# Two orders swapped in a normalise-and-feed-forward stream: centring before the mean on TensorE, squaring before the logarithm on ScalarE

## The chip, the cores and the metric

The kernel runs on one core of one Trainium2 chip. The metric is the time of one execution on the device, in microseconds. Five engines matter: TensorE (PE, matmuls into PSUM), VectorE (DVE), ScalarE (ACT), GpSimd (POOL) and SyncE (SP, which only starts transfers here). Each works off its own instructions in order, and they meet through semaphores.

## The reference, cut to what matters

The input is `x`, 16 images of 48 channels and 64 x 64 pixels, f32. There are two layers, each with a convolution-like mixer and a feed-forward part on the tokens (pixels):

```
x = x + L0_conv(ln_c(x))          # one of 4 experts: depthwise 3x3, gelu, 1x1
t = t + L0_ffn(ln_t(t))           # 48 -> 192 -> 48, relu, values rounded to an 8-bit and a 16-bit float
x = x + L1_conv(ln_c(x))          # cosine transform, layer norm, a state-space scan on four quarters, transform back
t = t + L1_ffn(ln_t(t))
```

Both `ln_c` and `ln_t` normalise each pixel over its 48 channels: `(v - mean(v)) / sqrt(var(v) + eps)`. The feed-forward part of either layer, and the norm in front of the first layer's mixer, are what the change is in.

## The kernel before

Two images of 48 channels make a pair on 96 partitions, so there are eight pairs (`PAIRS`), each 96 x 4096. A hardware loop runs over seven of them (`pair(p, False)`), and the last stands behind it (`pair(7, True)`). In a pair the second layer's mixer is computed (turning, cosine transform, scan, transform back), with the expert convolution of the next pair woven into the scan. After it comes a **stream**, the piece that the change touches.

A stream works through chunks of 512 pixels (`CH`), eight to an image pair. In a pair of the loop it has 24 of them: eight of the second layer's feed-forward (`ffn1`, source `x`), eight of the next pair's first feed-forward (`ffn0`, source `col`), and eight of the norm of the pair after that (`norm`, source `xin`). The stream of the last pair has eight (`ffn1`). In front of the loop there is one of eight (`norm`) and one of 16 (`ffn0`, `norm`). So 200 chunks are normalised in all.

Each chunk goes through these steps; the numbers are lines of the profile:

- TensorE multiplies it by `centre` (identity less the mean over channels), L547, into PSUM bank 0 or 1 (`LN_DEPTH` = 2 banks): the centred values.
- ScalarE squares them, L880, into `sq`.
- TensorE multiplies `sq` by `average`, L540, into PSUM bank 2 or 3: the variance.
- ScalarE takes the logarithm, L869, and `exp(-0.5 * .)` of it, L874: the inverse root.
- VectorE multiplies the centred values by it: L1191 in a feed-forward chunk (into `xq8`, 8 bits), L1199 in a norm chunk, there with a sum over the chunk, L1202. This counts up `normed`.
- In a feed-forward chunk TensorE applies the first layer, L559, three matmuls into banks 4 to 6. ScalarE copies them out, L887. VectorE adds the bias and clips, L1212 and L1214, and rounds to 8 bits, L1231. TensorE applies the second layer, L570, bank 7. VectorE copies it out, L1183, and adds its bias, L1222. GpSimd adds the residual, L1403.
- In the last iterations of a stream with `ffn0`, blocks of the new `x` are centred and turned: L523 on TensorE (eight matmul records a block), L856 and L857 on ScalarE.

The order is written out by hand. Each engine has its own function `stream`, a loop over `t` in which step k of the chain is done for chunk `t - k`, so that several chunks are under way. VectorE's iteration is L1183 of t-4, L1191 or L1199 of t-1, L1212 and L1214 of t-2, L1222 of t-4, L1231 of t-2. Waits are written as `wait_ge(semaphore, count)`, with `n = n0 + t` counting chunks over the whole kernel. The wait of the centring on `normed` guards its PSUM bank:

```
pe.wait_ge(normed, n - LN_DEPTH + 1)
```

For chunk t it asks that chunk t-2 has been multiplied. `settled` is a no-operation behind a group of waits.

Of the kernel before, what the change touches and what calls it, by code (L numbers as in the profile page):

```python
# [18 lines left out]
ACT = mybir.ActivationFunctionType  # L19
# [3 lines left out]
R = 2 * C  # L23
PX = H * W
PAIRS = B // 2
CH = 512
NCH = PX // CH
# [38 lines left out]
LN_DEPTH = 2  # L66
# [6 lines left out]
def program(nc, a):  # L73
# [3 lines left out]
    def sb(name, shape, dt=F32):  # L77
        return ctx.enter_context(nc.sbuf_tensor(name, shape, dt))

    def sem(name):  # L80
        return ctx.enter_context(nc.semaphore(name))

    with ctx:

        ident = sb("ident", [128, 128])
        centre = sb("centre", [R, R])
# [51 lines left out]
        def cut(rows, n, dt=F32, at=None):  # L138

            if at is None:  # L140
                at = top[0]
                top[0] += n
            v = arena[0:rows, at:at + n]
            return v if dt == F32 else v.bitcast(dt)
# [5 lines left out]
        sq = cut(R, LN_DEPTH * CH).rearrange("p (b n) -> p b n", b=LN_DEPTH)  # L150
# [50 lines left out]
        ps = ctx.enter_context(nc.psum_tensor("ps", [128, 8, 512], F32))  # L201
# [23 lines left out]
        centred = sem("centred")  # L225
        squared = sem("squared")
        averaged = sem("averaged")
        logged = sem("logged")
        rstd_ready = sem("rstd_ready")
        normed = sem("normed")  # L230
# [114 lines left out]
        def turned_in(parts, t):  # L345

            n = t - len(parts) + 6
            return n if "ffn0" in parts and 0 <= n < NG else None

        def is_ffn(parts, t):  # L350
            return 0 <= t < len(parts) and parts[t] != "norm"
# [30 lines left out]
        def settled(eng):  # L382


            eng.nop(nofuse=True)
# [111 lines left out]
        def _(pe):  # L497
# [7 lines left out]
            def turn_in(P, n):  # L505

                c = IN_ORDER[n]
                if n == 0:
                    pe.wait_ge(hf_ready, P * 2 * NCH + NCH)
                if n == 3:  # L510
                    pe.wait_ge(yf_ready, P * 2 * NCH + NCH)
                if n >= 4:
                    pe.wait_ge(pix_act, P * ACT_PAIR + act_before(T_IN) + n - 3)
                    settled(pe)
                    pe.wait_ge(ln_act, P * LN_ACT + A_SQUARE + n - 4)
                    settled(pe)
                if n == 4:
                    pe.wait_ge(centre_ready, P + 1)
                    settled(pe)
                pe.wait_ge(ffn_done, P * 2 * NCH + c + 1)  # L520
                for g in range(GB):
                    px = (c * GB + g) * 128
                    mm = pe.matmul(ps[:, 4 + n % 4, g * R:(g + 1) * R], x[:, px:px + 128], centre[:],  # L523
                                   start=True, stop=True)
                mm.then_inc(pix_ps, 1)
                if n == 1:

                    pe.wait_ge(ln_act, P * LN_ACT + A_SQUARE)
                    pe.matmul(centre_ps, sel_centre[:], pix[:, GRP // 2, :], start=True,
                              stop=True).then_inc(cen_ps, 1)  # L530

            def stream(n0, f0, parts, ready, src, P):

                for t in range(len(parts) + 3):
                    if 0 <= t - 1 < len(parts):
                        j, n = (t - 1) % NCH, n0 + t - 1
                        pe.wait_ge(squared, n + 1)
                        if not (parts[0] == "norm" and t - 1 < LN_DEPTH):
                            pe.wait_ge(logged, n - LN_DEPTH + 1)
                        pe.matmul(ps[0:R, LN_DEPTH + j % LN_DEPTH, :], average[:], sq[:, j % LN_DEPTH, :],  # L540
                                  start=True, stop=True).then_inc(averaged, 1)
                    if t < len(parts):
                        j, n = t % NCH, n0 + t
                        ready(t)
                        if not (parts[0] == "norm" and t < LN_DEPTH):
                            pe.wait_ge(normed, n - LN_DEPTH + 1)
                        pe.matmul(ps[0:R, j % LN_DEPTH, :], centre[:], src[parts[t]][:, j * CH:(j + 1) * CH],  # L547
                                  start=True, stop=True).then_inc(centred, 1)
                    if is_ffn(parts, t - 2):
                        j = t - 2  # L550
                        layer = int(parts[j] == "ffn1")
                        pe.wait_ge(normed, n0 + j + 1)
                        if j == 0:
                            ready(NCH - 1)
                        if j > 0:
                            pe.wait_ge(hf_ready, f0 + j)
                        settled(pe)
                        for b in range(3):
                            mm = pe.matmul(ps[:, 4 + b, :], w1[:, layer, b, :], xq8[:, j % 2, :],  # L559
                                           start=True, stop=True)  # L560
                        mm.then_inc(fc1_ready, 1)
                    if is_ffn(parts, t - 3):
                        j = t - 3
                        layer = int(parts[j] == "ffn1")
                        pe.wait_ge(h8_ready, f0 + j + 1)
                        if j > 0:
                            pe.wait_ge(yf_ready, f0 + j)
                        settled(pe)
                        for b in range(3):
                            mm = pe.matmul(ps[0:R, 7, :], w2[:, layer, b, :],  # L570
                                           h8[:, j % 2, b * CH:(b + 1) * CH],
                                           start=(b == 0), stop=(b == 2))
                        mm.then_inc(fc2_ready, 1)
                    if turned_in(parts, t) is not None:
                        turn_in(P, turned_in(parts, t))
# [30 lines left out]

            pe.wait_ge(x_in, 16)
            stream(0, 0, ("norm",) * NCH, lambda t: None, {"norm": xin}, None)
            router(1)
            pe.wait_ge(expert_ready, 1)  # L610
            for t in range(NCH + 1):
                if t < NCH:
                    if t >= 4:
                        pe.wait_ge(gelu_ready, t - 3)
                    for k in range(TAPS):
                        mm = pe.matmul(ps[0:R, t % 4, :], diag[:, k, :],
                                       taps_of(padded[:, t * ROWS:t * ROWS + ROWS + 2, :], k),
                                       start=(k == 0), stop=(k == TAPS - 1))
                    mm.then_inc(taps_ps, 1)
                if t >= 1:  # L620
                    j = t - 1
                    pe.wait_ge(gelu_ready, j + 1)
                    if j >= 4:
                        pe.wait_ge(pwb_ready, j - 3)
                    pe.matmul(ps[0:R, 4 + j % 4, :], pw_gated[:], gel0[:, j % 2, :],
                              start=True, stop=True).then_inc(pw_ps, 1)
# [216 lines left out]
        def _(act):  # L843
# [15 lines left out]
            def stream(n0, f0, parts, P):  # L859

                for t in range(len(parts) + 2):
                    if 0 <= t - 1 < len(parts):
                        k, n = (t - 1) % LN_DEPTH, n0 + t - 1
                        e = int(parts[t - 1] != "norm")
                        old = not (parts[0] == "norm" and t - 1 < LN_DEPTH)
                        act.wait_ge(averaged, n + 1)
                        if old:
                            act.wait_ge(rstd_ready, n - LN_DEPTH + 1)
                        act.activation(lnv[:, k, :], ps[0:R, LN_DEPTH + k, :], ACT.Ln,  # L869
                                       bias=eps[0:R, e:e + 1]).then_inc(logged, 1)  # L870
                        act.wait_ge(logged, n + 1)
                        if old:
                            act.wait_ge(normed, n - LN_DEPTH + 1)
                        act.activation(rstd[:, k, :], lnv[:, k, :], ACT.Exp, scale=-0.5).then_inc(rstd_ready, 1)  # L874
                    if t < len(parts):
                        k, n = t % LN_DEPTH, n0 + t
                        act.wait_ge(centred, n + 1)
                        if not (parts[0] == "norm" and t < LN_DEPTH):
                            act.wait_ge(averaged, n - LN_DEPTH + 1)
                        act.activation(sq[:, k, :], ps[0:R, k, :], ACT.Square).then_inc(squared, 1)  # L880
                    if is_ffn(parts, t - 2):

                        j = t - 2
                        act.wait_ge(fc1_ready, f0 + j + 1)
                        if j >= 2:
                            act.wait_ge(hr_ready, 2 * (f0 + j - 1))
                        act.activation(hf[:, j % 2, :], ps[:, 4:7, :].rearrange("p b n -> p (b n)"),  # L887
                                       ACT.Copy).then_inc(hf_ready, 1)
                    if turned_in(parts, t) is not None:
                        turn_in(P, turned_in(parts, t))  # L890
# [25 lines left out]
            for t in range(NCH + 1):  # L916
# [6 lines left out]
                if t >= 1:  # L923
                    j = t - 1
# [683 lines left out]
```

## Time and profile before

| | |
|---|---|
| three runs, median (lowest to highest) | 4641.31 us (4617.7 to 4661.02) |
| profiled execution | 4614.75 us, of which the span from first to last instruction is 4612.9 |
| busy: TensorE, VectorE, ScalarE, GpSimd | 87%, 77%, 64%, 54% of the span |
| mean granted TensorE clock | 0.922 of full speed |
| chunks in all streams | 200 (8, 16, seven times 24, 8) |

"Busy" is time in which an instruction of the engine was running. A start in the timeline is the moment at which its waits are over. An f32 matmul of 512 columns shows as two records, so 200 means are 400 records of L540.

### The profile page before, as it was taken

To read this page: it belongs to the slowest core of one execution; us is meant where nothing else is said; L and a number is where in the kernel's file an instruction comes from. 1 tells how busy PE (TensorE), PEld (TensorE's weight loads), DVE (VectorE), ACT (ScalarE), POOL (GpSimd) and SP (SyncE) were. 2 spreads that over 40 slices of the span, in tenths; PEclk is the share of its full clock that TensorE was granted. 3 is DMA by queue.
4 is the path that set the end of the run, shared out by engine and by line. 5 is a ranking of instruction groups with operands and counts; after the bars stand their busy time and mean duration, and the time that the engine had idled before them with its cause. 6 is when DMAs were issued, how large, how long until landed. Compare 5 with 4: busy or idle time off the path is not lost.

```text
span 4612.9 us, 49417 instructions
## 1 busy us (share of the span) xinstructions
PE 4009.5 (87%) x14248; PEld 1461.2 (32%) x14248; DVE 3563.9 (77%) x3093; ACT 2959.8 (64%) x3572; POOL 2483.7 (54%) x1148
## 2 busy tenths in 40 slices
PE   6779986899869998699986999779997799868997
PEld 2322233322332223322243222432233222332223
DVE  1469967699668996599965998659977699667996
ACT  2567756677566766577665675667757677565664
POOL 0237742577416873177731777227752477425774
PEclk9889998899989999799997999979999899987888
DMA  1147741577316763277623775347751577406661
GB/s 41 42 115 185 175 118 43 150 175 185 92 45 173 179 169 76 64 184 173 159 69 83 177 179 133 83 101 174 184 134 44 125 187 173 112 15 148 160 158 51
DMA packets 166836, 580.22 MB, mean 126 GB/s; under 512 B 22460, under 2 KB 23208, under 8 KB 162952
## 3 DMA queue, kind: packets, MB, share of 16 engines
q1 hardware_dynamic: 152168, 538.66, 47.6%
q10 hardware_dynamic: 14336, 37.76, 2.8%
q8 instruction: 132, 2.16, 0.2%
q14 instruction: 200, 1.64, 0.1%
HBM read 467.12 MB, written 71.48 MB: 117 GB/s over the span
## 4 chain that ended last, share of the span: by engine, by line
PE 56%; DVE 18%; issue 14%; ACT 8%; DMA 2%; POOL 1%; DVEq 0%; SPq 0%; ACTq 0%; POOLq 0%
PE ps L725 12%; PE ps L744 7%; PE ps L790 6%; DVE ps L1357 6%; PE ps L679 5%; DVE arena L1362 5%; PE ps L597 3%; PE ps L540 3%; PE ps L753 2%; PE ps L736 2%; PE ps L703 2%; PE ps L711 2%; ACT arena L887 2%; PE ps L695 2%; PE ps L687 2%
## 5 line engine op out<-in xcount | busy, mean ns | idle before, releaser
L1449 POOL TENSOR_TENSOR arena<-arena 128x1024 f32<-128x1024 f32 x768 | 1855.7, 2422 | 745.4 <-DVE arena L1362 744.8
L1362 DVE TENSOR_TENSOR_SCAN arena<-arena,ps 128x1024 f32<-128x1024 f32 x768 | 1756.1, 2287 | 98.4 <-ACT arena L1050 3.4
L1050 ACT ACTIVATE arena<-arena,a_all 128x1024 f32<-128x1024 f32 x768 | 873.0, 1141 | 340.7 <-DVE arena L1362 246.9
L1357 DVE TENSOR_TENSOR ps<-ps,arena 128x1024 f32<-128x1024 f32 x768 | 930.3, 1211 | 147.1 <-PE ps L727 146.2
L725 PE MATMUL ps<-arena,spread 32*128 32x512 f32 x1536 | 897.4, 672 | 96.7 <-DVE arena L1362 71.8
L727 PE MATMUL ps<-arena,spread 32*128 32x512 f32 x1536 | 883.6, 673 | 0.0
L744 PE MATMUL ps<-arena,gather 128*32 128x512 f32 x3072 | 536.4, 647 | 3.3 <-POOL arena L1449 2.3
L790 PE MATMUL ps<-x 96*96 96x512 f32 x1008 | 498.5, 612 | 0.0
L725 PEld LDWEIGHTS ps<-arena,spread 32*128 32x128 f32 x1536 | 233.0, 190 | 727.7 <-issue 420.2
L679 PE MATMUL ps<-arena,w_in 96*96 96x512 f32 x512 | 289.7, 718 | 37.0 <-DMA arena<-xq 37.0
L1403 POOL TENSOR_TENSOR x<-x,arena 96x512 f32<-96x512 f32 x64 | 113.9, 1780 | 369.1 <-DVE arena L1222 369.1
L1015 ACT ACTIVATE arena<-ps 128x512 f32<-128x512 f32 x128 | 76.4, 597 | 311.7 <-PE ps L711 311.7
L790 PEld LDWEIGHTS ps<-x 96*96 96x96 f32 x1008 | 143.1, 162 | 331.5 <-issue 331.5
L540 PE MATMUL ps<-arena,average 96*96 96x512 f32 x400 | 218.9, 629 | 30.8 <-ACT arena L880 30.8
L845 ACT ACT_TABLE_LOAD x178 | 228.4, 1283 | 23.9 <-DMA wo<-in_wo 20.7
L1439 POOL TENSOR_TENSOR arena<-arena 96x1024 f32<-96x1024 f32 x64 | 150.8, 2357 | 164.3 <-DVE arena L1347 164.3
L744 PEld LDWEIGHTS ps<-arena,gather 128*32 128x32 f32 x3072 | 107.8, 115 | 395.1 <-issue 312.7
L727 PEld LDWEIGHTS ps<-arena,spread 32*128 32x128 f32 x1536 | 227.7, 190 | 0.0
L1347 DVE TENSOR_TENSOR arena<-arena 96x1024 f32<-96x1024 f32 x64 | 76.8, 1199 | 186.4 <-ACT arena L1036 186.4
L869 ACT ACTIVATE arena<-ps,eps 96x512 f32<-96x512 f32 x200 | 136.4, 682 | 125.2 <-PE ps L540 125.2
L1429 POOL MEMSET arena<- 96x6 f32 x8 | 0.8, 103 | 400.5 <-ACT xq L966 400.5
L1191 DVE TENSOR_TENSOR arena<-ps,arena 96x512 fp8e5<-96x512 f32 x128 | 86.9, 679 | 128.6 <-ACT arena L874 128.3
(160 smaller groups left out, 5758.2 us busy)
## 6 DMA issues: line engine op xcount, KB each, us to landing
arena<-dl SPq DMA_DIRECT2D x768, 512.0 KB, 5.3
dl<-arena ACTq DMA_DIRECT2D x64, 384.0 KB, 5.1
x<-pn SPq DMA_DIRECT2D x56, 247.5 KB, 5.0
arena<-in_x SPq DMA_DIRECT2D x9, 1536.0 KB, 14.7
arena<-xq SPq DMA_DIRECT2D x64, 192.0 KB, 6.1
arena<-arena ACTq DMA_DIRECT2D x64, 192.0 KB, 4.7
out<-x SPq DMA_DIRECT2D x64, 192.0 KB, 2.1
arena<-xq SPq DMA_DIRECT2D x64, 191.8 KB, 5.4
```

The costliest lines, as they stand in the source:

```text
L540: pe.matmul(ps[0:R, LN_DEPTH + j % LN_DEPTH, :], average[:], sq[:, j % LN_DEPTH, :], start=True, stop=True).then_inc(averaged, 1)
L679: mm = pe.matmul(ps[0:DI, 6 + c, :], w_in[:, q, j, :], xs[:, i, c * 512 + 2 * j:c * 512 + 2 * j + 512], start=(j == 0), stop=(j == 1))
L725: pe.matmul(ps[:, bank, :], spread[rows[0], r, :], u[rows[0], i, 0:512], start=True, stop=True)
L727: pe.matmul(ps[:, bank + 1, :], spread[rows[1], r, :], u_low[rows[1], i, :], start=True, stop=True).then_inc(ubc_ready, 1)
L744: mm = pe.matmul(ps[b * BLK:(b + 1) * BLK, c, :], gather[:, r, :], hs[:, (r * TRIO + b) % HSS, c * 512:(c + 1) * 512], start=False, stop=( ...
L790: mm = pe.matmul(ps[0:R, 7, :], diag[:, k, :], taps_of(win[:, v % 2], k), start=(k == 0), stop=(k == TAPS - 1), skip_group_check=True)
L845: exp_table = lambda: act.preload_act_table_set("natural_log_exp_and_others")
L1050: act.activation(da[:, m % DAS, :], dbc[:, m % DBC, :], ACT.Exp, scale=a_all[:, v // 2, m:m + 1]).then_inc(da_ready, 1)
L1357: dve.tensor_tensor(driven, driven, bmat[:, v % 2, :], ALU.mult).then_inc(bu_ready, 1)
L1362: dve.tensor_tensor_scan(hs[:, m % HSS, :], da[:, m % DAS, :], driven, 0.0, ALU.mult, ALU.add).then_inc(h_ready, 1)
L1439: pool.tensor_tensor(u[:, i, :], delta, xi[:, i, :], ALU.mult).then_inc(u_ready, 1)
L1449: pool.tensor_tensor(product, product, cmat[:, v % 2, :], ALU.mult).then_inc(pr_ready, 1)
```

## The change

On TensorE the centring of chunk t, with its waits, is put in front of the mean of chunk t-1. On ScalarE the square of chunk t, with its waits, is put in front of the logarithm and root of chunk t-1. VectorE, GpSimd and SyncE are left as they are, and so are all the waits themselves.

```
@@ tensor: stream
                 for t in range(len(parts) + 3):
+                    if t < len(parts):
+                        j, n = t % NCH, n0 + t
+                        ready(t)
+                        if not (parts[0] == "norm" and t < LN_DEPTH):
+                            pe.wait_ge(normed, n - LN_DEPTH + 1)
+                        pe.matmul(ps[0:R, j % LN_DEPTH, :], centre[:], src[parts[t]][:, j * CH:(j + 1) * CH],
+                                  start=True, stop=True).then_inc(centred, 1)
                     if 0 <= t - 1 < len(parts):
                         j, n = (t - 1) % NCH, n0 + t - 1
                         pe.wait_ge(squared, n + 1)
...
                         pe.matmul(ps[0:R, LN_DEPTH + j % LN_DEPTH, :], average[:], sq[:, j % LN_DEPTH, :],
                                   start=True, stop=True).then_inc(averaged, 1)
-                    if t < len(parts):
...
-                        pe.matmul(ps[0:R, j % LN_DEPTH, :], centre[:], src[parts[t]][:, j * CH:(j + 1) * CH],
-                                  start=True, stop=True).then_inc(centred, 1)
@@ scalar: stream
                 for t in range(len(parts) + 2):
+                    if t < len(parts):
+                        k, n = t % LN_DEPTH, n0 + t
+                        act.wait_ge(centred, n + 1)
+                        if not (parts[0] == "norm" and t < LN_DEPTH):
+                            act.wait_ge(averaged, n - LN_DEPTH + 1)
+                        act.activation(sq[:, k, :], ps[0:R, k, :], ACT.Square).then_inc(squared, 1)
                     if 0 <= t - 1 < len(parts):
...
                         act.activation(rstd[:, k, :], lnv[:, k, :], ACT.Exp, scale=-0.5).then_inc(rstd_ready, 1)
-                    if t < len(parts):
-                        k, n = t % LN_DEPTH, n0 + t
...
-                        act.activation(sq[:, k, :], ps[0:R, k, :], ACT.Square).then_inc(squared, 1)
```

## Rows read from the trace of the kernel before

**Rows 1.** The page's part 4, chain that ended last: shares of the span by engine.

```profile
PE 56%; DVE 18%; issue 14%; ACT 8%; DMA 2%; POOL 1%; DVEq 0%; SPq 0%; ACTq 0%; POOLq 0%
```

**Rows 2.** Busy time by engine around one stream; PEclk is the granted clock.

```profile
670.00:787.00 117.00, 87.04 (x359) 45.24 (x357) 85.44 (x163) 78.32 (x117) 31.45 (x20) 0.93 0.20 57
```

**Rows 3.** Timeline, feed-forward part: start, us, engine, line; idle before it and releaser.

```profile
701.36 0.68 ACT L869 ACTIVATE arena<-ps,eps 96x512 f32<-96x512 f32 x1 [0.73 <-PE ps L540]
...
702.46 0.68 DVE L1183 CAST arena<-ps 96x512 f16<-96x512 f32 x1
...
703.24 0.82 PE L570 MATMUL ps<-arena,w 128*96 128x512 fp8e5 x3 [0.41 <-DVE arena L1183]
703.89 0.59 PE L540 MATMUL ps<-arena,average 96*96 96x512 f32 x1
...
704.75 1.02 PE L547 MATMUL ps<-col,centre 96*96 96x512 f32 x2
...
704.96 0.68 ACT L869 ACTIVATE arena<-ps,eps 96x512 f32<-96x512 f32 x1 [0.44 <-PE ps L540]
...
705.67 0.63 ACT L874 ACTIVATE arena<-arena 96x512 f32<-96x512 f32 x1
706.21 0.57 ACT L880 ACTIVATE arena<-ps 96x512 f32<-96x512 f32 x1
...
706.68 1.44 ACT L887 ACTIVATE arena<-ps 128x1536 f16<-128x1536 f32 x1
...
708.15 0.48 DVE L1212 TENSOR_SCALAR arena<-arena,b 128x1024 f16<-128x1024 f16 x1 [0.53 <-ACT arena L887]
...
709.95 0.68 DVE L1183 CAST arena<-ps 96x512 f16<-96x512 f32 x1
```

**Rows 4.** Timeline, the start of the same stream, its first chunk.

```profile
675.35 1.10 PE L540 MATMUL ps<-arena,average 96*96 96x512 f32 x2 [0.76 <-ACT arena L880]
...
676.29 1.02 PE L547 MATMUL ps<-x,centre 96*96 96x512 f32 x2
...
676.49 0.68 ACT L869 ACTIVATE arena<-ps,eps 96x512 f32<-96x512 f32 x1 [1.19 <-PE ps L540]
677.21 0.63 ACT L874 ACTIVATE arena<-arena 96x512 f32<-96x512 f32 x1
...
677.94 0.69 DVE L1191 TENSOR_TENSOR arena<-ps,arena 96x512 fp8e5<-96x512 f32 x1 [3.48 <-ACT arena L874]
```

**Rows 5.** Timeline, norm part of the same stream, its last two chunks.

```profile
755.43 0.68 ACT L869 ACTIVATE arena<-ps,eps 96x512 f32<-96x512 f32 x1 [0.42 <-PE ps L540]
...
756.15 0.63 ACT L874 ACTIVATE arena<-arena 96x512 f32<-96x512 f32 x1
...
756.81 0.69 DVE L1199 TENSOR_TENSOR arena<-ps,arena 96x512 f32<-96x512 f32 x1 [1.61 <-ACT arena L874]
...
758.45 0.68 ACT L869 ACTIVATE arena<-ps,eps 96x512 f32<-96x512 f32 x1 [0.42 <-PE ps L540]
```

**Rows 6.** Timeline behind that stream: a matmul that waits for VectorE.

```profile
769.27 0.27 DVE L1240 TENSOR_SCALAR pool_lhs<-pool_mask,pooled 96x96 f32<-96x96 f32 x1
...
769.59 0.48 PE L580 MATMUL ps<-router_w,pool_lhs 96*96 96x4 f32 x2 [9.43 <-DVE pool_lhs L1240]
```

**Rows 7.** Timeline of the first stream of all (norm chunks only).

```profile
32.19 0.68 ACT L869 ACTIVATE arena<-ps,eps 96x512 f32<-96x512 f32 x1 [2.11 <-PE ps L540]
...
34.54 2.02 PE L540 MATMUL ps<-arena,average 96*96 96x512 f32 x2 [0.68 <-ACT arena L880]
...
36.36 1.91 PE L547 MATMUL ps<-arena,centre 96*96 96x512 f32 x2
...
36.60 0.68 ACT L869 ACTIVATE arena<-ps,eps 96x512 f32<-96x512 f32 x1 [2.11 <-PE ps L540]
```

**Rows 8.** Timeline of TensorE in the scan of the last pair.

```profile
4358.18 0.81 PE L725 MATMUL ps<-arena,spread 32*128 32x512 f32 x1 [1.41 <-DVE arena L1362]
...
4358.78 1.06 PE L725 MATMUL ps<-arena,spread 32*128 32x512 f32 x1
```

More of the change, by code:

```diff
@@ L541, in stream @@
                                   start=True, stop=True).then_inc(averaged, 1)
-                    if t < len(parts):
[L543 to L546, printed above, removed]
-                        pe.matmul(ps[0:R, j % LN_DEPTH, :], centre[:], src[parts[t]][:, j * CH:(j + 1) * CH],
-                                  start=True, stop=True).then_inc(centred, 1)
                     if is_ffn(parts, t - 2):
@@ L874, in stream @@
                         act.activation(rstd[:, k, :], lnv[:, k, :], ACT.Exp, scale=-0.5).then_inc(rstd_ready, 1)
-                    if t < len(parts):
-                        k, n = t % LN_DEPTH, n0 + t
-                        act.wait_ge(centred, n + 1)
-                        if not (parts[0] == "norm" and t < LN_DEPTH):
-                            act.wait_ge(averaged, n - LN_DEPTH + 1)
-                        act.activation(sq[:, k, :], ps[0:R, k, :], ACT.Square).then_inc(squared, 1)
                     if is_ffn(parts, t - 2):
```

## The prediction

> **What bounds the kernel now.** I read the page's chain of waits first [rows 1]: it runs through TensorE for 56% of the span, through VectorE for 18% and through ScalarE for 8%, so it changes engine all the time and the bound differs by stage. The diff touches `stream` alone, so I went on to the busy times around one stream and saw 87 of 117 us on TensorE, 85 on VectorE and 78 on ScalarE, at a granted clock of 0.93 [rows 2]. Nobody is full there, so a ring of waits sets the pace, and the timeline has to be walked.
>
> In the feed-forward part [rows 3] I start at a VectorE copy of the second layer's output (L1183, at 702.46) and follow what waits for what. The second layer's matmuls start 0.78 later (703.24). Behind them in TensorE's order stands the mean (L540, 703.89: 0.65). Its logarithm starts at 704.96 (1.07), the root at 705.67 (0.71), the square of the next chunk at 706.21 (0.54), the copy of the first layer's output (L887) 0.47 after that, the VectorE steps on that copy at 708.15 (1.47), and the next but one L1183 at 709.95 (1.80). One turn takes 709.95 - 702.46 = 7.49 us and covers two chunks: 3.745 us a chunk. In the norm part a shorter ring binds, that of mean, logarithm, root, square and mean: logarithm to logarithm is 758.45 - 755.43 = 3.02 us [rows 5].
>
> The square does stand in both rings, and its centred input is there before ScalarE comes to it. That is what the change addresses.
>
> **What it changes.** No instruction is added or removed: there are 200 centring matmuls, 200 means, 200 squares, logarithms and roots before and after. The orders change. ScalarE now does square(t), logarithm(t-1), root(t-1). TensorE now does centre(t), mean(t-1). No DMA moves, and the queues of SyncE and GpSimd stay as they are. The wait that matters moves with the matmul: centre(t) waits for normed(t-2), since the centred values lie in two PSUM banks. Before, mean(t-1) stood ahead of that wait. Now it stands behind it, and so do the first layer of chunk t-2 and the second layer of chunk t-3.
>
> That closes a new ring with a period of one chunk: centre(t), mean(t-1), logarithm(t-1), root(t-1), the VectorE multiply of chunk t-1, centre(t+1). Its links come from the rows:
> - centre to mean: 0.94, the distance of two such matmuls of which the first found TensorE idle (675.35 to 676.29) [rows 4]. Both are 512 columns of f32 on 96 rows. With TensorE busy it would be 0.86 (703.89 to 704.75) [rows 3], but the centring always waits here.
> - mean to logarithm: 1.07, the mean coming right behind other matmuls [rows 3].
> - logarithm to root: 0.71 [rows 3]. Root to multiply: 0.73 in the feed-forward part (677.21 to 677.94) [rows 4], 0.66 in the norm part (756.15 to 756.81) [rows 5].
> - multiply to centring: 0.74. The multiply takes 0.69. The handover from VectorE to TensorE is not shown for this pair, so I take the nearest row, 0.05 (769.27 + 0.27 to 769.59) [rows 6]. The 0.78 of L1183 to L570 [rows 3] has a settling nop in it and is the upper end.
>
> The sum is 4.19 us a chunk in the feed-forward part and 4.12 in the norm part. Bounds: 4.11 with 0.86 for the first link, 4.23 with 0.78 for the last.
>
> Does something else end later? I lay one turn out from centre(t) = 0. Mean 0.94; the square is ready to run at 1.14 (the delay behind a lone matmul, 675.35 to 676.49) [rows 4] and frees ScalarE at 1.61; logarithm 2.01; root 2.72; multiply 3.45; L887 at 2.72 + 0.54 = 3.26; the steps on it at 4.73; L1183 at 6.53. It leads to the next multiply 0.60 later, at 7.13, against the 7.64 that the ring asks for. The second layer starts at 6.53 - 4.19 + 0.78 = 3.12 and is over at 3.77, before 4.19. Everything fits with some 0.4 us to spare, so the new ring is the bound. The old ring does not shrink either: its square (0.54) leaves and a centring (0.86) enters, because the second layer is now followed by centre and only then by mean. That gives 7.49 - 0.54 + 0.86 = 7.81, or 3.9 a chunk, above 3.745 as well.
>
> Now the sum, logarithm to logarithm:
> - A full stream (24 chunks, seven of them) takes 758.45 - 676.49 = 81.96 us now. The first logarithm stays where it is. After it come 16 turns of 4.19 (67.04) and 6 of 4.12 (24.72). The last chunk has no centring ahead of its mean. Its logarithm follows when TensorE has turned one more block and ScalarE has done its root and the two copies of that block, about 2.0. Together 93.8, so +11.8 each, **+82.7** in all.
> - The stream in front of the loop (16 chunks) has eight feed-forward turns fewer: 11.8 - 8 x (4.19 - 3.745) = **+8.2**, an estimate that leaves out a short slow stretch at its start.
> - The last stream (8 chunks, feed-forward only) takes 701.36 - 676.49 = 24.87 for its seven distances [rows 3, 4]. Six turns of 4.19, then 2.83 (the last mean waits for the second layer, 3.77 - 0.94) make 27.97: **+3.1**.
> - The first stream of all (8 norm chunks) runs on slow matmuls, 1.82 apart, with 2.06 from mean to logarithm and 4.41 a chunk [rows 7]. Its new ring is 1.82 + 1.99 + 0.71 + 0.66 + 0.74 = 5.92, where 1.99 is 2.06 less the 0.07 by which 1.07 is under 1.14. That is six times +1.51; about 0.9 at the start, since the first mean now follows two centrings (3.64) and not one and its square (2.06 and some 0.6); and 1.8 in place of 4.41 for the last: **+7.3**.
>
> This is +101 us. What could hide it? The streams stand between stages that all wait for their last chunk: VectorE goes on with its large sums as soon as the last chunk is normed. The spill of `x` and the store of the normed image are issued from the stream's own events and have the following stage to land. I count no cover.
>
> **The clock.** The matmuls of the stream take 0.59 us (or 1.02 for two) [rows 3, 4], the upper of the two levels (2.4 GHz); those of rows 7 take 1.91 for two, the lower (1.2 GHz). In the last scan a matmul pair that came after an idle time of 1.41 us took 0.81 us, and the one behind it 1.06 [rows 8]: the clock had fallen to the lower level. In a new stream TensorE idles 0.7 and 0.4 in each turn of the feed-forward part, and some 1.5 us a turn in the norm part (centre, mean and eight turning matmuls fill 2.6 of 4.12). At the start, before any first layer, the second mean waits about 2.4 us. So I expect the clock to fall at the start of about half of the streams, one turn each at the lower level, and dense matmuls to bring it back: 4 x 1.8 = +7. The bounds of this term are 0 and the second rival below. The Trainium skill (TensorE: Matmul & The Clock Gate, Why this matters for your kernels) warns only of idle gaps longer than any of these; by its rule the term is nothing and the sum ends at +101. The fall behind a 1.41 us gap speaks against relying on it.
>
> **Forecast.** 101 + 7 = 108 us. The profiled execution took 4614.75, of which the span is 4612.9, and would become 4723. The median of the three runs is 27 above that, at 4641, so the forecast is 4749, slower by 2.3%.
>
> **Rivals.**
> 1. *The ring with the square is cut and nothing takes its place* (faster). The feed-forward ring would lose 0.54: 6.95 / 2 = 3.48 a chunk, 0.27 less on some 120 turns, -32. The norm part would go from 3.02 to TensorE's own 2.65 (two times 0.86 and a block of turning matmuls, 0.9) on some 50 turns, -18. Time 4591. Against it is the wait on `normed` ahead of centre(t), and the sum of its ring. It decides if that ring is shorter than 3.745, and no link has 0.45 us to give. 4%.
> 2. *The clock falls in the norm part and stays.* Then a norm turn costs 5.92 and not 4.12: 1.8 x 6 in eight streams is +86, time 4835. For it: idle gaps of 1.5 us each turn, just the size of that in rows 8, and the first stream of all, which never left slow matmuls while turning at 4.41 [rows 7]. Against it: the norm part holds the full clock now, and eight turning matmuls fill every turn. A partial form of it, two or three turns in some streams, gives 4780. 20% together.
> 3. *The delay is taken up outside the streams or the change does not act* (within 1%, at most 4687). A wait on a transfer or a branch at the end of the stream would have to hide 60 of 101 us. All eight stages behind a stream begin with work on its last chunk. 6%.
> 4. *The handovers are quicker than my rows* and the old ring of 3.9 binds: 0.28 less on 120 feed-forward turns, -34, time 4715. It lies inside the forecast's range.
>
> **Chances.** Forecast with rival 4 70%, rival 2 20%, rival 3 6%, rival 1 4%. The range goes from 4700 (rival 4 and some of the 43 us over which the runs before spread) to 4820, which takes in half of rival 2. A measurement of this kernel tells about 1% from no change. Faster by over 1%: 0.04. Within 1%: 0.06. Slower by over 1%: 0.90.
>
> **What would show it.** Right: logarithms 4.1 to 4.2 us apart in both parts of a stream, a full stream of about 94 us, the centring matmul with an idle time before it that ends with the multiply (L1191 or L1199), and the mean 0.94 behind it. Wrong: a distance of 3.5 (rival 1) or 3.9 (rival 4); matmul durations of 1.0 to 1.1 us in the norm part (rival 2); a span that grows by much less than the streams do (rival 3). What would spoil the forecast is a clock that behaves otherwise at gaps of 1.5 to 2.4 us, or a shift of the scans by some us that changes their own clock.

## The result, and the profile after

The changed kernel takes 4789.92 us in the median of four runs (4780.93 to 4801.09), the kernel before 4630.19 in its four (4617.7 to 4661.02). The ratio is 1.0336, 95% interval 1.0275 to 1.0397: slower by 3.4%, or 160 us. The forecast was 4749 us, with a range of 4700 to 4820. The profiled execution took 4793.87 us with a span of 4792.1, against 4614.75 and 4612.9 before: 179 us more. Its mean granted clock is 0.899, against 0.922.

Three parts of the page answer to [rows 1]: the busy times, the chain of waits by engine, and two of the costliest groups with the idle time ahead of them.

```profile
PE 4118.4 (86%) x14248; PEld 1489.8 (31%) x14248; DVE 3570.8 (75%) x3093; ACT 2983.2 (62%) x3572; POOL 2487.4 (52%) x1148
...
PE 59%; DVE 17%; issue 12%; ACT 8%; DMA 2%; POOL 1%; DVEq 0%; SPq 0%; POOLq 0%; ACTq 0%
...
L867 ACT ACTIVATE arena<-ps 96x512 f32<-96x512 f32 x200 | 118.4, 592 | 244.9 <-PE ps L540 244.9
L1191 DVE TENSOR_TENSOR arena<-ps,arena 96x512 fp8e5<-96x512 f32 x128 | 87.9, 686 | 232.9 <-ACT arena L880 232.9
```

The counts are those of before, so no work was added. The multiply L1191 now waits 232.9 us for the root (L880), where it waited 128.3 before, and the square L867 waits 244.9 us for the centring (L540), where it waited 68.3. The groups of centring matmuls by source and shape say what those wait for:

```profile
L540 PE MATMUL ps<-x,centre 96*96 96x512 f32 x128 | 74.4, 676 | 44.5 <-DVE arena L1191 44.5
L540 PE MATMUL ps<-col,centre 96*96 96x512 f32 x128 | 73.8, 662 | 31.6 <-DVE arena L1191 29.3 <-POOL col L1410 2.3
L540 PE MATMUL ps<-arena,centre 96*96 96x512 f32 x144 | 90.8, 718 | 61.3 <-DVE arena L1199 49.8 <-DVE arena L1191 6.5 <-DMA arena<-in_x 5.1
```

That is 137 us of idle TensorE, nearly all of it ended by the multiply (L1191 or L1199); before, the centring followed on 7 us in all, none of it ended by the multiply. The centring matmuls are also longer than at full clock: a record of one on `x` took 592 ns before and takes 676 now, a mean over two clock levels.

The timeline of the first full stream shows both effects. The five rows from 697.86 are its start, the seven from 735.44 the feed-forward part (beside [rows 3]), and the last five the norm part (beside [rows 5]).

```profile
697.86 0.68 ACT L875 ACTIVATE arena<-ps,eps 96x512 f32<-96x512 f32 x1 [0.33 <-PE ps L547]
...
699.31 0.69 DVE L1191 TENSOR_TENSOR arena<-ps,arena 96x512 fp8e5<-96x512 f32 x1 [3.48 <-ACT arena L880]
...
700.14 1.96 PE L540 MATMUL ps<-x,centre 96*96 96x512 f32 x2 [2.31 <-DVE arena L1191]
...
701.89 1.91 PE L547 MATMUL ps<-arena,average 96*96 96x512 f32 x2
...
703.84 0.68 ACT L875 ACTIVATE arena<-ps,eps 96x512 f32<-96x512 f32 x1 [1.11 <-PE ps L547]
...
735.44 0.68 ACT L875 ACTIVATE arena<-ps,eps 96x512 f32<-96x512 f32 x1 [0.27 <-PE ps L547]
...
736.16 0.63 ACT L880 ACTIVATE arena<-arena 96x512 f32<-96x512 f32 x1
...
736.52 0.82 PE L570 MATMUL ps<-arena,w 128*96 128x512 fp8e5 x3 [0.47 <-DVE arena L1183]
...
736.92 0.69 DVE L1191 TENSOR_TENSOR arena<-ps,arena 96x512 fp8e5<-96x512 f32 x1 [0.50 <-ACT arena L880]
...
737.66 1.10 PE L540 MATMUL ps<-col,centre 96*96 96x512 f32 x2 [0.32 <-DVE arena L1191]
...
738.60 1.02 PE L547 MATMUL ps<-arena,average 96*96 96x512 f32 x2
...
739.65 0.68 ACT L875 ACTIVATE arena<-ps,eps 96x512 f32<-96x512 f32 x1 [0.27 <-PE ps L547]
...
784.51 1.10 PE L540 MATMUL ps<-arena,centre 96*96 96x512 f32 x2 [1.29 <-DVE arena L1199]
...
785.45 1.84 PE L547 MATMUL ps<-arena,average 96*96 96x512 f32 x2
...
787.33 0.68 ACT L875 ACTIVATE arena<-ps,eps 96x512 f32<-96x512 f32 x1 [1.09 <-PE ps L547]
...
789.45 2.02 PE L540 MATMUL ps<-arena,centre 96*96 96x512 f32 x2 [0.50 <-DVE arena L1199]
...
793.21 0.68 ACT L875 ACTIVATE arena<-ps,eps 96x512 f32<-96x512 f32 x1 [1.12 <-PE ps L547]
```

Read one turn from 735.44 on. The root follows the logarithm by 0.72, the multiply the root by 0.76, the centring the multiply by 0.74, the mean the centring by 0.94, and the next logarithm the mean by 1.05. The sum is 4.21 us, where one chunk took 3.745 before. This is the ring that was forecast, link by link. The second layer (L570) starts inside it and ends none of its waits.

At the start of the stream the same ring runs on slow matmuls: centring and mean take 1.96 and 1.91 us (two records each), and the logarithms are 703.84 - 697.86 = 5.98 apart. In the norm part the clock falls during the mean at 785.45 (1.84), and the logarithms are 793.21 - 787.33 = 5.88 apart. The windows over these three stretches show the granted clock in the column behind POOL's:

```profile
696.00:710.00 14.00, 10.65 (x16) 2.89 (x15) 3.08 (x5) 6.52 (x10) 0.00 (x0) 0.65 0.19 46
713.00:775.00 62.00, 49.03 (x144) 16.44 (x143) 46.72 (x89) 47.23 (x59) 25.05 (x14) 1.00 0.09 26
785.00:803.00 18.00, 17.00 (x42) 9.61 (x41) 4.96 (x10) 8.87 (x16) 1.99 (x2) 0.51 0.16 54
```

A clock of 1.00 is the upper level (2.4 GHz), 0.51 the lower (1.2 GHz). TensorE seems full in the third window (17.00 of 18.00 us), yet only because each matmul lasts nearly twice as long.

From each stream's first logarithm to its last, all streams together took 683.6 us before and take 837.8 now: +154 of the +179. A full stream took 81.96. Two of the seven now take 96.8, the other five 99.3 to 104.6.

### The profile page after: what moved, and what is told of

Same layout as the page of the kernel before. It is cut to its first block, busy times and chain, and to the rows that moved or that the text cites. A ratio compares the mean times of both kernels' runs of the same rounds, so it can differ in the third digit from the quotient of the medians.

```text
span 4792.1 us, 49417 instructions
## 1 busy us (share of the span) xinstructions
PE 4118.4 (86%) x14248; PEld 1489.8 (31%) x14248; DVE 3570.8 (75%) x3093; ACT 2983.2 (62%) x3572; POOL 2487.4 (52%) x1148
## 4 chain that ended last, share of the span: by engine, by line
PE 59%; DVE 17%; issue 12%; ACT 8%; DMA 2%; POOL 1%; DVEq 0%; SPq 0%; POOLq 0%; ACTq 0%
PE ps L725 11%; PE ps L744 7%; PE ps L790 6%; DVE ps L1357 6%; PE ps L679 5%; PE ps L540 5%; DVE arena L1362 4%; PE ps L547 4%; PE ps L597 3%; ACT arena L875 3%; PE ps L753 2%; ACT arena L880 2%; PE ps L703 2%; PE ps L736 2%; PE ps L711 2%
## 5 line engine op out<-in xcount | busy, mean ns | idle before, releaser
L867 ACT ACTIVATE arena<-ps 96x512 f32<-96x512 f32 x200 | 118.4, 592 | 244.9 <-PE ps L540 244.9
L1191 DVE TENSOR_TENSOR arena<-ps,arena 96x512 fp8e5<-96x512 f32 x128 | 87.9, 686 | 232.9 <-ACT arena L880 232.9
L547 PE MATMUL ps<-arena,average 96*96 96x512 f32 x400 | 238.8, 683 | 0.0
```

## The experiments

Each kernel was timed against the kernel before on the same chip. "Streams" is the sum over all ten streams of the time from first to last logarithm, from the profiled execution. In the edits, `centre(t)` and the like stand for the statements of that step.

**TensorE's swap alone.** The kernel before with centre(t) ahead of mean(t-1) in TensorE's order; ScalarE as before.

```diff
 for t in range(len(parts) + 3):      # TensorE
+    centre(t)      # waits for normed(t-2)
     mean(t-1)
-    centre(t)
```

> Only TensorE's order is changed (centring of t ahead of the mean of t-1); ScalarE keeps logarithm, root, square. Theory: the new ring is centre(t), mean(t-1), logarithm, root, multiply, centre(t+1), and ScalarE's order is no part of it. So this edit alone gives nearly the whole loss: logarithms 4.2 us apart in the feed-forward part and 4.1 in the norm part, time 4740 to 4800, as the full change. Rival: the loss needs the square ahead of the logarithm (ScalarE waiting for the centring before it does the logarithm); then this kernel stays within 1% of the 4630 before, or in the middle at about 4700.

It took 4817.74 us, a ratio of 1.0419 (1.0375 to 1.0464), 18 us above the range that I expected. The feed-forward logarithms are 4.21 to 4.28 apart, as in the full change, so the moved wait alone makes the ring. The norm distances are 4.12 at full clock, but mostly 5.89 (here at the lower level):

```profile
786.48 0.68 ACT L869 ACTIVATE arena<-ps,eps 96x512 f32<-96x512 f32 x1 [2.40 <-PE ps L547]
...
788.60 2.02 PE L540 MATMUL ps<-arena,centre 96*96 96x512 f32 x2
...
790.41 1.91 PE L547 MATMUL ps<-arena,average 96*96 96x512 f32 x2
...
792.36 0.68 ACT L869 ACTIVATE arena<-ps,eps 96x512 f32<-96x512 f32 x1 [3.31 <-PE ps L547]
```

The streams sum to 877.6 us, more than in the full change (837.8), since the clock is low for more of the norm turns. Added to this, ScalarE's swap takes nothing from the ring. It shortens the last distance of a stream (1.99 against 3.01 at full clock).

**ScalarE's swap alone.** The kernel before with square(t) ahead of logarithm(t-1) and root(t-1) in ScalarE's order; TensorE as before.

```diff
 for t in range(len(parts) + 2):      # ScalarE
+    square(t)      # waits for centred(t)
     logarithm(t-1); root(t-1)
-    square(t)
```

> Only ScalarE's order is changed (square of t ahead of the logarithm of t-1); TensorE keeps mean, centre. Theory: the logarithm of t-1 now waits for the square of t and so for the centring of t, which TensorE does behind the mean. Norm part: ring centre, square, logarithm, root, multiply, centre = 1.07 + 0.47 + 0.71 + 0.66 + 0.74 = 3.65 us a chunk. Feed-forward part: the old ring with 0.86 + 1.07 + 0.47 in place of 1.07 from mean to logarithm, less the square, is about 8.35 for two chunks, 4.18 each. Over 120 and 48 chunks that is +52 and +30, time 4700 to 4740. Rival: squaring early only helps, since the centred input was waiting (the intent of the change); then 4630 or less.

It took 4784.45 us, a ratio of 1.034 (1.0302 to 1.0379), well above the 4700 to 4740 expected. The feed-forward part came as expected: the distances alternate between 4.38 and 3.97, a mean of 4.175. The norm part did not. In all seven full streams its last full turns are 5.07 apart, behind two of about 7.1 and 5.5. In the one below, the clock fell behind an idle time of 1.84 us in which TensorE waited for a VectorE copy (L1183), at the change from feed-forward to norm. The timeline of one such turn, and the windows ahead of it and over it:

```profile
773.55 0.67 ACT L875 ACTIVATE arena<-ps,eps 96x512 f32<-96x512 f32 x1
...
774.47 1.92 PE L540 MATMUL ps<-arena,average 96*96 96x512 f32 x2
...
776.17 1.91 PE L547 MATMUL ps<-arena,centre 96*96 96x512 f32 x2
777.88 1.86 PE L523 MATMUL ps<-centre,x 96*128 96x96 f32 x8
...
778.62 0.67 ACT L875 ACTIVATE arena<-ps,eps 96x512 f32<-96x512 f32 x1
```

```profile
715.00:760.00 45.00, 34.32 (x110) 13.23 (x107) 34.28 (x65) 34.26 (x44) 19.52 (x11) 1.00 0.09 27
765.00:790.00 25.00, 25.00 (x62) 14.24 (x62) 6.43 (x12) 11.91 (x25) 2.43 (x3) 0.50 0.20 65
```

Mean, centring and turning start 1.70, 1.71 and 1.65 apart and fill the turn: at the lower level TensorE itself is the bound. It is busy for 25.00 of 25.00 us and the clock does not come back. In the 16-chunk stream the clock stayed up, and there the distance was 3.74, close to the ring of 3.65 that I had worked out. So the ring was right and the clock was the miss, as in the prediction itself. This swap loses by another ring than the full change: the logarithm of t-1 waits behind the square of t, and so for a centring that TensorE does behind the mean.

**A third bank for the centred values.** The full change, but centred chunks rotate through three PSUM banks, and the fourth holds every mean. centre(t) now waits for normed(t-3), and mean(t-1) for the logarithm before it. The control is the kernel before with the same banks.

```diff
-pe.wait_ge(normed, n - LN_DEPTH + 1)     # centre(t)
-pe.matmul(ps[0:R, j % LN_DEPTH, :], ...)
+pe.wait_ge(normed, n - 3 + 1)
+pe.matmul(ps[0:R, t % 3, :], ...)
-pe.wait_ge(logged, n - LN_DEPTH + 1)     # mean(t-1)
-pe.matmul(ps[0:R, LN_DEPTH + j % LN_DEPTH, :], ...)
+pe.wait_ge(logged, n)
+pe.matmul(ps[0:R, 3, :], ...)
```

> The changed kernel with three PSUM banks for centred chunks (0 to 2) and one for the mean (3), so that the centring of t waits for the multiply of t-3 and not t-2. Theory: this cuts the new ring. The feed-forward part then runs at the old ring with a centring in place of the square, 3.9 us a chunk (+20 over the kernel before), the norm part at 2.7 (-15), and the long idle time of TensorE at the start of a stream is gone. Time 4620 to 4660. Rival: the loss comes from the means standing later in TensorE's order or from the clock by itself; then the third bank takes back less than half of the 160 us, time over 4710.

> Control: the kernel before with the same three banks for centred chunks and one for the mean. Theory: no ring that bounds it goes through a centred bank or a second mean bank, so nothing changes: logarithms 3.745 and 3.02 us apart, time 4615 to 4650. Rival: the bank layout is worth something by itself (then it is faster or slower by over 1%, and the kernel with the new orders and three banks has to be read against this one).

The changed orders with three banks took 4617.11 us, a ratio of 0.9978 (0.9955 to 1.0001). The control took 4633.03, 1.0008 (0.9989 to 1.0027), with the distances of before. The expected ranges were 4620 to 4660 and 4615 to 4650. One bank more gives the whole loss of the change back and gives nothing to the old order. It is the wait on `normed`, at a depth of two, that costs. In the timeline the centring comes well ahead of its use:

```profile
698.80 1.02 PE L541 MATMUL ps<-col,centre 96*96 96x512 f32 x2
699.66 1.02 PE L548 MATMUL ps<-arena,average 96*96 96x512 f32 x2
700.73 0.68 ACT L876 ACTIVATE arena<-ps,eps 96x512 f32<-96x512 f32 x1 [0.27 <-PE ps L548]
700.97 0.68 DVE L1184 CAST arena<-ps 96x512 f16<-96x512 f32 x1
701.75 0.82 PE L571 MATMUL ps<-arena,w 128*96 128x512 fp8e5 x3 [0.42 <-DVE arena L1184]
702.40 1.02 PE L541 MATMUL ps<-col,centre 96*96 96x512 f32 x2
...
704.33 0.68 ACT L876 ACTIVATE arena<-ps,eps 96x512 f32<-96x512 f32 x1 [0.27 <-PE ps L548]
...
708.59 0.68 ACT L876 ACTIVATE arena<-ps,eps 96x512 f32<-96x512 f32 x1 [0.27 <-PE ps L548]
```

TensorE now waits for L1184, the copy of the second layer's output. The distances alternate, 3.60 and 4.26: the old feed-forward ring with the square out and a centring in, at the 3.9 a chunk of the prediction's layout. The norm part goes down to 2.58 (a full stream also has one turn of 2.81 and one of 3.48), and the first stream takes 14.39 us in place of 30.87. The streams sum to 665.9 us, 18 less than before. But 16.5 of these 18 are the first stream, and mostly its clock: a mean took 1.02 to 1.17 us there, against 2.02 before [rows 7]. A full stream takes 82.4 us, no less than the 81.96 of before. In the profiled executions the time outside the streams is 18 us longer, so that nothing is left in the end.

**TensorE kept busy: four kernels against the clock.** To separate the clock from the ring I gave TensorE work that changes no result. In the first, the turning blocks 0 to 4 of a stream's norm part are done twice into the same place. In the second, two more centrings follow the first mean and one follows the second, into a bank that nobody reads before it is written again. The third has both.

```diff
-for g in range(GB):
+for g in tuple(range(GB)) * (2 if n <= 4 else 1):     # turning
 ...
     mean(t-1)
+    for _ in range(3 - t):     # t is 1 or 2; not in the stream of norm chunks alone
+        pe.matmul(ps[0:R, 7, :], centre[:], src[parts[0]][:, 0:CH], start=True, stop=True)
```

> The changed kernel, with the eight matmuls of each of the turning blocks 0 to 4 of a stream done twice into the same bank before they are reported (0.86 us more work in each of five norm turns; the result is the same). The ring of the norm part does not run through them and has 1.5 us of idle TensorE time a turn. Theory: it is this idle time that lets the clock fall near the end of five of the seven full streams; with 0.65 left the clock holds, all norm distances are 4.12 and not up to 5.9, and the last one is 1.99 in all streams. That takes 22 us off the profiled streams: time 4755 to 4775, faster than the changed kernel in spite of more work. Rival: the clock falls for another reason and the extra work only costs; then 4790 or more.

> The changed kernel, with two matmuls of 0.86 us into an unused bank behind the first mean of a stream with a feed-forward part, and one behind the second mean (nothing reads them). Theory: the idle time of 2.3 us between the first mean and the third centring makes the clock fall in all eight such streams; with it filled, the first two distances of a stream are 4.2 to 4.3 each and not 5.0 to 6.0. About 2.3 us a stream, 19 in all: time 4765 to 4780. Rival: the clock falls later, at the second or third turn, where some 1.7 us are still idle; then only the place of the slow turns moves and the time stays at 4790.

> The changed kernel with both fillers, at the start of each stream and in five norm turns. Theory: inside the streams the clock then stays at its upper level, a full stream takes about 96 us in all seven places, and what is left against the 82 us before is the ring alone. If only the streams count: 4735 to 4755. Rival: the time saved in a stream comes back in the stage behind it, whose own clock depends on when the stream ends, as the start filler alone has shown (16 us less in the streams of the profiled run, none in the time); then 4765 to 4785.

With turning doubled: 4773.19 us, 1.0306 (1.0273 to 1.0339). In the eight streams that have turning blocks every norm distance is 4.12 and every last one 1.99, for one turn of 5.5 instead of 4.6; the streams sum to 820.1. With the start filled: 4795.46, 1.0344 (1.031 to 1.0379). The first distances are 4.25 (4.18 in the 16-chunk stream) and the streams sum to 821.9, but the time did not follow, against what I expected (4765 to 4780): outside the streams the profiled execution is 16 us longer than the change (3970.7 against 3954.2). With both: 4748.85, 1.0249 (1.0216 to 1.0282), all seven full streams alike at 96.3 us, 801.0 in sum. The windows of the third kernel, the first two in the places of those after the change, the last over the end of the same stream:

```profile
696.00:710.00 14.00, 11.70 (x31) 3.94 (x31) 5.06 (x9) 9.31 (x13) 0.00 (x0) 1.00 0.14 34
713.00:775.00 62.00, 49.89 (x157) 18.16 (x156) 46.31 (x88) 45.51 (x58) 26.36 (x15) 1.00 0.09 27
775.00:793.00 18.00, 16.62 (x93) 11.50 (x92) 6.43 (x12) 12.38 (x23) 2.15 (x2) 1.00 0.28 90
```

The first window has a clock of 1.00 where the change had 0.65, the last 1.00 where the change had 0.51 at the end of its stream. The kernel with 187 more matmuls in it (374 records) is 41 us faster than the change, which is the clock's part that such fillers can take back, net of their own cost. What is left over the kernel before is 113 us.

The fourth kernel goes the other way: the mean stands behind the first layer, so that a feed-forward turn holds 0.65 us more for the same work.

```diff
     centre(t)
-    mean(t-1)
     first_layer(t-2)
+    mean(t-1)
     second_layer(t-3)
```

> The changed kernel with the mean of t-1 put one step later still on TensorE, behind the first layer of t-2 (0.64 us of matmuls at the full clock). Nothing else moves. Theory: the new ring takes in whatever TensorE does between centring and mean, so each feed-forward turn grows by 0.65, from 4.2 to 4.85, and the norm turns, which have no first layer, stay at 4.12. About 120 turns: +78 on the 4790 of the changed kernel, 4850 to 4880. Rival: the ring is not what sets the pace in the feed-forward part (a ring through the second layer or the output copies is); then the 0.65 is hidden in TensorE's idle time of 1.1 us a turn and the time stays at 4790.

It took 4940.03 us, 1.0645 (1.0592 to 1.0698).

```profile
746.49 1.10 PE L540 MATMUL ps<-col,centre 96*96 96x512 f32 x2 [1.03 <-DVE arena L1191]
...
748.08 1.02 PE L560 MATMUL ps<-arena,average 96*96 96x512 f32 x2
749.14 0.68 ACT L875 ACTIVATE arena<-ps,eps 96x512 f32<-96x512 f32 x1 [0.91 <-PE ps L560]
...
754.00 0.68 ACT L875 ACTIVATE arena<-ps,eps 96x512 f32<-96x512 f32 x1 [0.92 <-PE ps L560]
...
756.56 1.51 PE L540 MATMUL ps<-col,centre 96*96 96x512 f32 x2 [1.32 <-DVE arena L1191]
```

The distance at full clock is 4.86 = 4.21 + 0.65: whatever stands between centring and mean is paid in full, as it must be in a ring. The time came out above what I expected (4850 to 4880): the clock now falls in the feed-forward part too, where slow turns of 6.2 to 7.3 us stand among those of 4.9, behind idle times of about 1 us in each turn (1.03 ahead of the centring here, then 1.32 ahead of the first slow one). The streams sum to 970.9 us.

**The feed-forward ring of before, shortened.** Both kernels have two FFN steps moved: TensorE's second layer runs at t-4 instead of t-3, and VectorE multiplies chunk t-1 ahead of its copy of the second layer's output. The first keeps the orders and banks of before; the second has the changed orders and three banks.

```diff
-if is_ffn(parts, t - 3):      # TensorE, second layer
-    j = t - 3
+if is_ffn(parts, t - 4):
+    j = t - 4
 for t in range(1, len(parts) + 4):      # VectorE
-    copy_second_layer(t-4)
     multiply(t-1)
+    copy_second_layer(t-4)
```

> The kernel before, without the change, but with the old feed-forward ring opened: TensorE does the second layer of chunk t-4 and not t-3, and VectorE does the multiply of t-1 ahead of the copy of t-4. The ring of 7.49 us for two chunks ran through the wait of the mean behind the second layer, which waited for VectorE's copy. Theory: with one chunk more between them that wait is over before TensorE comes to it, and VectorE's own work is what is left, 0.60 + 0.67 + 0.67 + 0.26 + 0.87 = 3.07 us a chunk against 3.745. On 120 feed-forward chunks that is -80, less one more iteration at the end of each stream: time 4545 to 4590. Rival: other rings of about 3.7 are just behind (logarithm, root, square and copy on ScalarE add up to 3.05, TensorE 3.0), or the clock falls; then 4600 to 4630.

> The same opening of the feed-forward ring in the changed kernel with three banks for centred chunks. Theory: with the ring through the centring cut, the changed orders cost nothing and give the norm part 2.6 us a chunk in place of 3.02; the feed-forward part is again VectorE's 3.07. Time 10 to 25 below the kernel with the old orders and this opening, 4525 to 4575. Rival: the changed orders keep the feed-forward part longer than 3.07 because the mean comes later; then it is slower than that kernel.

The first took 4538.84 us, 0.9807 (0.9772 to 0.9841), a little under the 4545 to 4590 expected; the second 4535.87, 0.9786 (0.9754 to 0.9817). Both beat both kernels of this case. In the first the feed-forward logarithms are 3.06 apart:

```profile
692.89 0.68 ACT L869 ACTIVATE arena<-ps,eps 96x512 f32<-96x512 f32 x1
...
694.16 0.81 PE L570 MATMUL ps<-arena,w 128*96 128x512 fp8e5 x3
...
695.95 0.68 ACT L869 ACTIVATE arena<-ps,eps 96x512 f32<-96x512 f32 x1
```

The second layer (L570) now follows without an idle time ahead of it, so the ring through both layers of the FFN, which held 3.745, is no longer the bound. With it gone, the changed orders with three banks make the streams 37 us shorter still (565.1 against 602.5 in sum; 16 of the 37 are the first stream, 2.1 each full one). But the medians are 3 us apart, not the 10 to 25 expected, and their intervals overlap. In the profiled executions the gain went into the stages between the streams, which last 475.5 to 481.4 us from last to next logarithm in most cases, against 474.7; why was not settled.

## Why the prediction was right, and where it was off

**The mechanism held.** That the wait on `normed`, moved ahead of the mean, closes a ring of one chunk's period is shown three ways. The timeline has its five links (4.21 against 4.19; 4.11 to 4.12 in the norm part against 4.12). TensorE's swap alone makes it, and a third bank takes it away. Of the +160 us, 108 were forecast; the time lies in the range because the range took in half of rival 2. Of the +179 of the profiled executions, 71 were not forecast: 9 of the ring, 37 of the clock in the streams and 25 outside them.

**Rivals 1 and 3 fell.** But for the last distance of the last stream (2.73, forecast as 2.83), none was below 3.745 in the feed-forward part, and nothing outside the streams hid any of the delay. Rival 4 (an old ring of 3.9) binds only once the new one is gone, as the third bank showed.

**The ring terms of the sum were 9 us short.** At full clock, as in the kernel with both fillers and less the turns that these lengthen, the streams would sum to about 794, which is +110 over before. Forecast was +101. A full stream takes 95.4 (the kernel with the start filled has two) and not 93.8. Most of it is the turns that touch the second FFN layer's chunks, 4.27 and not 4.19, and two longer ones, 4.56 at the change between the layers' chunks and 4.61 at the first turning block. I had laid out one feed-forward turn and taken it for all. The first stream gained 5.9 and not 7.3, the 16-chunk stream 6.8 and not 8.2, the last 3.5 at full clock and not 3.1.

**The step that was mis-sized is the clock term**, "4 x 1.8 = +7". The streams of the change are 837.8 - 794 = 44 us longer than at full clock. The fall at the start came in every stream behind the first and not in half of them, and often held for two turns. (The gap was there as forecast, 2.31 us, but ahead of the third centring and not of the second mean.) In five of seven full streams, and with TensorE's swap alone more often still, the clock also fell late in the norm part. That is the partial form of rival 2, to which I gave 20% together with the full form. Its price of 1.8 us a turn was right (5.89 against 4.12). My ground against it, that eight turning matmuls fill every turn, was wrong: the same matmuls held the clock at 3.02 a turn [rows 5] and lost it in five of seven streams at 4.12. With turning doubled it held in all of them. A longer ring thins TensorE's work, and that was the term to size. The single gap does not decide: in the two full streams that kept the clock, the norm turns have the same idle time of 1.29 us as at 784.51. What parts them from the other five is not shown.

**What the page's rule was worth.** The prediction set the warning of the Trainium skill (TensorE: Matmul & The Clock Gate, Why this matters for your kernels) against the row with 1.41 us. The trace does not bear the rule out as a bound: the clock was down behind 2.31 us at the start and behind norm turns with a gap of 1.3 us. The same page says, in Part 1: The HAM clock gate, that "activity releases the throttle". The norm part of the kernel with ScalarE's swap alone disagrees with that as it reads: busy for 25.00 of 25.00 us by the profile (which models the ends of matmuls), clock 0.50.

**Outside the streams.** Of the 179 us of the profiled executions, 25 lie between the streams. I counted nothing there. In the medians only 160 are lost in all: the profiled execution of before was 15 us under its median, that of the change 4 over. Stages behind a full stream differ in one kernel, too: 473.7 to 483.1 us in the change, and 474.1 to 474.7 in the same six places before. Two stages of 483 make up 17 of the 25. The part in which one of them (the lower line) falls most behind another of the same kernel (475.4 in all) lies in the scan, 100 to 115 us behind the end of the stream:

```profile
902.50:917.50 15.00, 15.00 (x45) 4.44 (x45) 14.44 (x10) 10.53 (x13) 10.28 (x5) 0.92 0.63 149
1474.70:1489.70 15.00, 15.00 (x32) 3.57 (x32) 10.26 (x6) 6.61 (x10) 9.15 (x4) 0.54 0.54 131
```

TensorE has work all the time in both, but at a clock of 0.54 it gets through 32 matmul records and not 45, and VectorE is busy for 10.26 us and not 14.44. Shortly before, a matmul of the slow stage had waited 5.68 us for a transfer, that of the other 3.03. That the moment at which a stream ends decides how the clock stands in the next stage fits this and the fruitless start fillers, but it is argued and not shown. No run moved a stream's end by itself.

## What to carry to other kernels

An engine's order is part of the buffering. A wait for a free buffer, put ahead of a step on which that same buffer's release depends, closes a ring. Walk the ring and add its links before moving anything; with one more buffer the same order can be harmless. When a ring gets longer, ask next how much work is left on TensorE per turn, since its clock may fall and nearly double every matmul in the ring. Last, look for the ring that binds now: here it ran through the second layer's place in the order, and moving that was worth 1.9%, where taking the square out was worth 0.2% even with a third bank, which is not clear of the noise (0.9955 to 1.0001).

## What the runs showed of the hardware

- The clock fell at gaps shorter than I had thought safe: in the norm part with 1.3 us idle in turns of 4.12 (in five full streams of seven), in the kernel with the mean behind the first layer with 1.0 and 0.5 us in turns of 4.86.
- More matmuls made the kernel faster: 4789.92 us without the fillers and 4748.85 with them.
- At the lower level TensorE can be busy by the profile without a break and stay there (25 us in the kernel with ScalarE's swap alone), while the same mean, centring and turning matmuls kept the full clock at 3.74 a turn in its 16-chunk stream.
- In the first stream of the kernel before, mean and centring ran at the lower level for all 31 us with 0.68 us idle in each turn of 4.41 [rows 7]. In the changed orders with three banks the same matmuls ran at the upper level there, with 0.2 to 0.3 us idle in every other turn.
- An f32 matmul of 512 columns (two records) takes 1.02 us at the upper level and 1.91 at the lower, and the distance from its start to the logarithm behind it grows from 1.05 to 1.95 (701.89 to 703.84).
